# A four-layer block on one core: groups of a quantised weight loaded ahead into free rows, page copies moved into the down stage

## The reference

```python
# layer 0: gated MLP with an adapter (rank 16) per sequence, F = 1376
gate = x @ W_gate.T + 0.5 * lora(x, A_gate, B_gate)
up   = x @ W_up.T   + 0.5 * lora(x, A_up, B_up)
x = x + (silu(gate) * up) @ W_down.T + 0.5 * lora(silu(gate) * up, A_down, B_down)

# layer 1: attention, 32 query and 8 key/value heads of 128, over 512 cached keys + 128 new ones
kc = k_cache[block_table].reshape(bsz, L, HK, D)      # 16 pages of 32 keys per sequence
vc = v_cache[block_table].reshape(bsz, L, HK, D)
x = x + softmax(mask(rope(rmsnorm(q)) @ k_all.T * SCALE)) @ v_all @ Wo.T

# layer 2: weight quantised to a codebook, per group of 128 inputs
delta = lora_B @ lora_A * 0.5
normalized = (weight + delta) / exp(scale_log)        # 4 groups
quantized = cb[searchsorted(thresholds, normalized)]
x = x + x @ ((quantized - normalized + normalized) * exp(scale_log) + delta).T

# layer 3: one of eight weights per sequence
x = x + einsum('bsi,boi->bso', x, weight[adapter_ids])
```

## Time and profile before

| | us |
|---|---|
| median of 3 runs | 1441.49 |
| lowest, highest | 1437.01, 1442.73 |
| profiled execution | 1439.98 |
| its span | 1438.4 |
| PE busy in it | 1378.1 (96%) |
| DVE, ACT, POOL busy | 1021.5, 977.4, 744.6 |

### The profile page before, as it was taken

How to read it: one execution, slowest core, us unless ns; L and a number is a source line. 1 busy time by engine, 2 the same in 40 slices (tenths; PEclk the granted TensorE clock), 3 DMA queues, 4 the chain that set the end, 5 groups by cost and what they waited for, 6 DMA issues and landing times.

```text
span 1438.4 us, 26330 instructions
## 1 busy us (share of the span) xinstructions
PE 1378.1 (96%) x7812; PEld 1190.9 (83%) x7812; DVE 1021.5 (71%) x2111; ACT 977.4 (68%) x1986; POOL 744.6 (52%) x986
## 2 busy tenths in 40 slices
PE   6899898889999999999999999999999999999888
PEld 5788776678888888888888888888888888888766
DVE  3787666467777777777777777777777777777656
ACT  4667564467777677777776777777777777777643
POOL 5322222376666566656555665565566656655300
PEclk9999999999999999999999999999999999999989
DMA  8788778356332424332332324232323242422144
GB/s 193 220 268 271 238 183 268 96 141 177 88 89 59 105 58 111 67 103 68 80 104 60 90 76 113 62 89 60 103 60 89 73 114 53 100 60 59 33 180 147
DMA packets 256596, 165.80 MB, mean 115 GB/s; under 512 B 157398, under 2 KB 223575, under 8 KB 250951
## 3 DMA queue, kind: packets, MB, share of 16 engines
q1 hardware_dynamic: 250928, 144.51, 37.3%
q0 software_dynamic: 5376, 19.60, 4.8%
q10 hardware_dynamic: 150, 0.01, 0.0%
HBM read 158.66 MB, written 38.94 MB: 137 GB/s over the span
## 4 chain that ended last, share of the span: by engine, by line
PE 74%; DVE 6%; issue 5%; ACT 5%; DMA 4%; POOL 3%; SPq 2%; POOLq 0%; DVEq 0%; ACTq 0%
PE proj_ps L1361 17%; PE sc L1401 13%; PE o_ps L1439 13%; PE ring L1419 8%; PE sc L1161 5%; PE proj_ps L1455 4%; PE proj_ps L1458 3%; PE proj_ps L1466 3%; PE o_ps L1161 3%; PE proj_ps L1161 2%; DMA prep<-scale_dram 2%; PE ring L1478 1%; DMA inv_row<-inv_dram 1%; SPq L333 1%; DVE bias L1904 1%
## 5 line engine op out<-in xcount | busy, mean ns | idle before, releaser
L1921 DVE TENSOR_TENSOR pTl<-ring,pTh 128x512 fp32r<-128x512 f32 x320 | 215.3, 689 | 145.0 <-ACT pTh L969 140.8
L958 ACT ACTIVATE p_sb<-p_sb,bias,rstd 128x640 f32<-128x640 f32 x256 | 235.3, 920 | 57.6 <-DVE bias L1904 57.6
L1888 DVE CUSTOM_DVE_ANT_0 p_sb<-sc,mask 128x640 f32<-128x640 f32 x256 | 206.5, 823 | 24.4 <-PE sc L1401 18.1
L704 POOL TENSOR_TENSOR rstd<-var,half_neg 128x4 f32<-128x4 f32 x64 | 65.1, 1017 | 301.5 <-DVE var L1953 301.5
L969 ACT ACTIVATE pTh<-ring 128x512 fp32r<-128x512 f32 x320 | 184.3, 599 | 28.5 <-PE ring L1419 27.0
L1419 PE MATMUL ring<-ident,p_sb 128*128 128x128 f32 x1280 | 182.3, 273 | 4.2 <-DVE pTl L1921 2.7
L1361 PE MATMUL proj_ps<-wh,xh 128*128 128x512 f32 (+1 forms) x512 | 179.5, 351 | 0.7 <-ACT q_sb L1005 0.7
L1361 PE MATMUL proj_ps<-wl,xh 128*128 128x512 f32 (+1 forms) x512 | 173.5, 339 | 6.9 <-DVE wl L1745 6.9
L1419 PEld LDWEIGHTS ring<-ident,p_sb 128*128 128x128 f32 x1280 | 153.5, 141 | 31.1 <-DVE pTl L1921 3.2
L1361 PE MATMUL proj_ps<-wh,xl 128*128 128x512 f32 (+1 forms) x512 | 172.4, 337 | 0.0
L1401 PE MATMUL sc<-kTh,qTh 128*128 128x320 f32 x512 | 163.3, 319 | 3.0 <-DVE kTl L1995 3.0
(11 more groups left out here) (244 smaller groups left out, 3602.4 us busy)
## 6 DMA issues: line engine op xcount, KB each, us to landing
k_pages<-in_k_cache SPq DMA_DIRECT2D x128, 128.0 KB, 3.5
v_pages<-in_v_cache POOLq DMA_DIRECT2D x128, 128.0 KB, 3.7
k_raw<-k_pages SPq DMA_DIRECT2D x256, 64.0 KB, 2.5
v_raw<-v_pages SPq DMA_DIRECT2D x64, 256.0 KB, 2.9
rope<-rope_dram SPq DMA_DIRECT2D x64, 256.0 KB, 3.4
inv_row<-inv_dram SPq DMA_DIRECT2D x64, 256.0 KB, 3.7
stage<-in_Wqkv SPq DMA_DIRECT2D x32, 384.0 KB, 4.5
w_raw<-in_WguT SPq DMA_DIRECT2D x19, 512.0 KB, 5.3
```

The costliest lines, as they stand in the source:

```text
L704: pool.tensor_tensor(rstd[:, u.k % 2, 0:REP], var[:, u.k % 2, 0:REP], half_neg[:, 0:REP], ALU.pow).then_inc(S["q_pow"], 1)
L958: act_e.activation(p_sb[:, p_slot(u, h), :], p_sb[:, p_slot(u, h), :], ACT.Exp, bias=bias[:, h:h + 1], scale=rstd[:, u.k % 2, h:h + 1], ac ...
L1888: v.tensor_tensor_reduce(out=p_sb[:, p_slot(u, h), :].rearrange("p (s k) -> p s k", s=2), in0=score_ps[h % 2][:, :, 0:SPLIT], in1=mask[:, ...
L1921: v.tensor_tensor(pTl[:, c, :], ring[c % 2][:, :], pTh[:, c, :].bitcast(F32), ALU.subtract).then_inc(S["ptl"], 1)
```

## The change

**Groups in rows of their own.** Group 0 stays in `prep` 0 to 2. Groups 1 and 3 go to rows 3 to 5 of `rope_tab`, seen as `spare`, group 2 to its rows 0 to 2. Results go to `prep` rows 2, 1, 0 and 2 (`made_row`). `load_group` stands at q = 11, 13, 16 and 20 and waits for the group before to have landed; group 3 also for `leaf_step` 5, which is stage 0 of group 2. `store_group` of groups 0 and 1 moves ahead of the page copies of q = 16 and 19, group 2's behind the last copies of the loop, group 3's to n = 6 of the down loop.

**x later.** The first half of x is loaded at q = 18 instead of 13, the second at n = 3 of the down loop instead of q = 16.

**Pages.** Key pages: `KEY_COPIES` gives 2 for q 6 to 10, 3 for 11 to 15, 5 for 16 to 21, then 5, then 5 per block of the down loop instead of 2, then 5 per step of attention. Value pages: 3 instead of 5 for iterations 11 to 15, then 28 instead of 18 after gate/up.

**The down stage.** The loads of the first attention unit move two blocks (`Wqkv`, keys), or one (values, tables, `Wo`) down. On DVE stage 1 of group 3 moves from ahead of block 2's split to behind it, stage 2 from k = 3 to 4. ACT's wait for the stored results moves from k = 5 to 7.

**SBUF.** `xh`, `woh`, `wol` and `w2_h`, `w2_l` change their places in the layout.

```diff
+KEY_COPIES = [0] * 6 + [2] * 5 + [3] * 5 + [5] * 6
+        def group_row(g, n):
+            return prep[:, n, :] if g == 0 else spare[:, 3 * (g % 2) + n, :]
+        def made_row(g):
+            return prep[:, (2, 1, 0, 2)[g], :]
...
                 else:
-                    sp.wait_ge(S["w2_ready"], g)
-                load(prep[:, 0, :], ins["W2T"][:, g, :], S["w2_in"])
+                    sp.wait_ge(S["w2_in"], 48 * g)
+                    if g == 1:
+                        sp.wait_ge(S["rope_in"], 16)
+                    if g == 3:
+                        sp.wait_ge(S["leaf_step"], 5)
+                load(group_row(g, 0), ins["W2T"][:, g, :], S["w2_in"])
...
-                if q == 13:
-                    load(x_sb[:, 0:HALF, :], ins["x"][0:HALF].rearrange("b t n -> t b n"), x_in[0])
-                if q == 16:
-                    sp.wait_ge(S["xl_set"], 2 * C)
-                    load(x_sb[:, HALF:, :], ins["x"][HALF:].rearrange("b t n -> t b n"), x_in[1])
+                if q in (13, 16, 20):
+                    load_group({13: 1, 16: 2, 20: 3}[q])
                 if 19 <= q:
                     load_wd(CH + q - 19)
-                copy_keys(2 if q < FC else 5)
-                if q in (16, 19, 21):
+                if q == 18:
+                    load(x_sb[:, 0:HALF, :], ins["x"][0:HALF].rearrange("b t n -> t b n"), x_in[0])
+                if q in (16, 19):
                     store_group(q // 3 - 5)
-                    load_group(q // 3 - 4)
+                copy_keys(KEY_COPIES[q])
             copy_keys(5)
...
-            for n in range(FC):
-                if n >= 3:
-                    load_wd(CH + n)
-                    copy_keys(2)
-                if n == 5:
-                    store_group(3)
-                if n == 2:
+            store_group(2)
+            for n in range(3, FC):
+                load_wd(CH + n)
+                if n == 3:
+                    sp.wait_ge(S["xl_set"], 2 * C)
+                    load(x_sb[:, HALF:, :], ins["x"][HALF:].rearrange("b t n -> t b n"), x_in[1])
+                copy_keys(5)
+                if n == 4:
                     sp.wait_ge(S["gate_up"], 4 * FC)
...
-                copy_values(4 if n < FC else 5)
+                copy_values(4 if n < FC else 3 if n < 16 else 5)
             pool.wait_ge(S["gate_up"], 4 * FC)
-            copy_values(18)
+            copy_values(28)
...
-                    if g:
-                        dve.wait_ge(S["put"], PUT_SCALES + 16 * g)
...
-            weight2(*STAGES[2 * FC - 1])
             first = Unit(0)
             for k in range(2, CH):
                 split_wd(CH + k)
                 if k == 2:
                     mask_t(1, 2)
                     low_t(1, 2)
-                if k == 3:
+                    weight2(*STAGES[2 * FC - 1])
+                if k == 4:
                     weight2(*STAGES[2 * FC])
```

More of the change, by code:

```diff
@@ L207, in cond_resid_kernel @@
         tb_raw = prep[0:PAIR, 8, :]
+        spare = rope_tab[:, :, :, :].rearrange("p k b d -> p (k b d)").rearrange("p (r n) -> p r n", n=HID)
         wd_b = [la_h[:, :, :, :].rearrange("p k c r -> p k (c r)"), act_h[:, 0:2, :]]
@@ L222, in cond_resid_kernel @@
         wl = l1_sb("wl", [P, C, QKV], F32R)
-        woh = l1_sb("woh", [P, REP, HID], F32R)
-        wol = l1_sb("wol", [P, REP, HID], F32R)
+        xh = l1_sb("xh", [P, B, C, T], F32R)
         rope = l1_sb("rope", [P, 2, 4, D])
@@ L227, in cond_resid_kernel @@
         v_raw = l1_sb("v_raw", [P, LC, D])
-        xh = l1_sb("xh", [P, B, C, T], F32R)
+        woh = l1_sb("woh", [P, REP, HID], F32R)
+        wol = l1_sb("wol", [P, REP, HID], F32R)
         xl = l1_sb("xl", [P, B, C, T], F32R)
@@ L269, in cond_resid_kernel @@
         w3_raw = l2_sb("w3_raw", [P, 2, C, HID])
+        w2_h = l2_sb("w2_h", [P, C, HID], F32R)
+        w2_l = l2_sb("w2_l", [P, C, HID], F32R)
         x2T_h = l2_sb("x2T_h", [P, 2, C * T], F32R)
@@ L274, in cond_resid_kernel @@
         w3_h = l2_sb("w3_h", [P, 2, C, HID], F32R)
-        w2_h = l2_sb("w2_h", [P, C, HID], F32R)
-        w2_l = l2_sb("w2_l", [P, C, HID], F32R)
         w3_l = l2_sb("w3_l", [P, 2, C, HID], F32R)
@@ L388, in load_group @@
                 else:
-                    sp.wait_ge(S["w2_ready"], g)
-                load(prep[:, 0, :], ins["W2T"][:, g, :], S["w2_in"])
-                load(prep[:, 1, :], scale_dram[0, g, :].partition_broadcast(P), S["w2_in"])
-                load(prep[:, 2, :], scale_dram[1, g, :].partition_broadcast(P), S["w2_in"])
+                    sp.wait_ge(S["w2_in"], 48 * g)
[4 more added lines that the diff above has]
+                load(group_row(g, 0), ins["W2T"][:, g, :], S["w2_in"])
+                load(group_row(g, 1), scale_dram[0, g, :].partition_broadcast(P), S["w2_in"])
+                load(group_row(g, 2), scale_dram[1, g, :].partition_broadcast(P), S["w2_in"])
             def store_group(g):
                 sp.wait_ge(S["w2_ready"], g + 1)
-                sp.dma_start(w2_dram[:, g, :], prep[:, 4, :]).then_inc(S["put"], 16)
+                sp.dma_start(w2_dram[:, g, :], made_row(g)).then_inc(S["put"], 16)
             load_x_chunk(0, 0)
@@ L486, in _ @@
                     load_k(first)
-                if n == 4:
+                if n == 5:
                     load_v(first)
@@ L490, in _ @@
                     load_rope(first)
-                if n in (6, 8):
-                    for h in (n - 6, n - 5):
+                if n == 6:
+                    store_group(3)
+                if n in (7, 9):
+                    for h in (n - 7, n - 6):
                         sp.wait_ge(S["wqkv_l"], h + 1)
@@ L526, in step @@
                     load_v(u + -1)
-                if 2 <= u.k < B - 1:
+                if u.k < B - 1:
                     copy_keys(2)
                 spread_inv(u + -2)
+                if u.k < 2:
+                    copy_keys(3)
                 if (u + 1).exists():
@@ L534, in step @@
                 load_next_out(u)
-                if u.k < B - 1:
-                    copy_keys(6 if u.k < 2 else 4)
+                if 2 <= u.k < B - 1:
+                    copy_keys(3)
             run_steps(step)
@@ L930, in _ @@
                 split_wd(CH + k)
-                if k == 5:
+                if k == 7:
                     act_e.wait_ge(S["put"], PUT_SCALES + 16 * C)
@@ L1702, in weight2 @@
             def weight2(g, stage):
-                w, scale, norm, delta = (prep[:, n, :] for n in range(4))
+                w, scale, norm = (group_row(g, n) for n in range(3))
+                delta = prep[:, 3, :]
                 tmp = w
@@ L1726, in weight2 @@
                     then(v.tensor_tensor(tmp, tmp, scale, ALU.mult))
-                    v.tensor_tensor(leaf[0], tmp, delta, ALU.add).then_inc(S["w2_ready"], 1)
+                    if g == 3:
+                        dve.wait_ge(S["put"], PUT_SCALES + 16)
+                    v.tensor_tensor(made_row(g), tmp, delta, ALU.add).then_inc(S["w2_ready"], 1)
             def low_act(n):
```

## The result

| | before | changed kernel |
|---|---|---|
| median of the runs | 1440.65 us (1437.01 to 1442.73, 4 runs) | 1455.33 us (1452.7 to 1457.98, 4 runs) |
| ratio, 95% interval | | 1.0113 [1.0095, 1.0132] |
| profiled execution | 1439.98 us | 1454.83 us |
| TensorE's first product of down block 1 | 227.76 us | 216.13 us |
| down stage ended (first product of attention) | 265.10 us | 279.93 us |

The changed kernel is slower by 1.1%, 14.7 us by the medians and 14.85 us in the profiled executions. The forecast was 1453 us, in a range of 1442 to 1461. TensorE enters the down stage 11.6 us earlier, leaves it 14.8 us later, and what follows (attention and the last two layers) takes as long as before: 1173.3 us from attention's first product to the end in both.

A forecast was written before the change was run, and what follows sets the result against it. SP's page copies at 1.25 us each were taken to delay the W_down blocks: 212.3 + 51.8 issues block 10 at 264.1, the stage ends at 276.7, +11.5 us, so 1441.5 + 11.5 = 1453 us, range 1442 to 1461.

The forecast's parts named there:

- What bounds: Whole run: TensorE works in nearly all of attention, so moving the down stage's end moves the run by as much.
- Part 1, -8.9 us: Gate/up: loading groups ahead removes DVE's scale-row waits and TensorE's resulting waits, so TensorE enters the down stage 8.9 us earlier.
- Part 2, at most -5.3: Down stage: weight2 behind the W_down split removes at most TensorE's 3.6 us wait and 1.7 us of low clock.
- Part 3, 1.25 us a page: SP queue, down loop: each page costs 1.25 us, so a block comes every 6.85 us or later; TensorE uses two in 5.75.
- The start, load 4 at 212.3: Down stage: load 4 waits for DVE's split of block 1, 10.0 us earlier at 212.3; SP arrives at the same moment, 211.6.
- The sum, 51.8 us to block 10: SP queue: issues and pages from load 4 take 51.8 us, so block 10 is issued at 264.1 instead of 254.76.
- "Six or seven us from one `wd_raw` issue to the next": SP queue, down stage: sign that the forecast is right; issues closer than 6 us would show it wrong.
- The tail, 12.5 us: Down stage after block 10's issue: 10.5 us as in the trace, plus 2 us for the late Wo loads.
- The end of the stage, 276.7: Down stage ends at 276.7 instead of 265.26, +11.5 us; bounds +6.5 and +16.
- What costs nothing: GpSimd's 28 value pages after gate/up end at 246, before the stage ends; fewer attention pages gain at most 1 or 2, taken as 0.
- The rival "faster": Down stage: the queue is no bound, TensorE alone sets the stage, ending at 250.7, a run of 1427; chance 0.12.
- Hold-ups like the 3.11 us: SP queue, down stage: rival slower by more, five transfer hold-ups of 2.5 us, +12.5 more, 1465; chance 0.06.

The follow-up runs named there:

- the nine kernels: The kernel before (1440.65 us), the changed kernel (1455.33 us) and the seven experiment kernels, measured from 1426.73 to 1464.63 us.
- the one with the low stretch at 122 us: Kernel with key pages at their old places, its 16 down-loop pages moved into the first half of gate/up: 1426.73 us, ratio to before 0.9934.
- the run with the old `weight2` order: Kernel with key pages at their old places, VectorE's two late weight2 steps put back ahead of the block 2 and 3 splits: 1429.33 us, ratio to before 0.9943.
- the run with fixed numbers: Changed kernel with the down loop's 40 page copies taken from constant page numbers, none read: 1436.91 us, ratio to before 0.9993.
- the run of the pages alone: Kernel before with only the key pages moved as in the change: 1464.63 us, ratio to before 1.0188.
- the first four experiments: Changed kernel with old key-page places 1429.99 us, small copies 1451.51, fixed page numbers 1436.91; kernel before with only key pages moved 1464.63.

## Why the prediction was right, step by step

**What bounds.** Right. A change of the down stage's end went through to the run one to one: 14.8 us at the stage's end, 14.8 in the span. That rests on what follows, which took 1173.3 us in both; that it agrees so closely is in part luck, since over the nine kernels it lies between 1168.3 and 1173.3 (last section).

**Part 1, -8.9 us.** (Its own terms make 8.8.) The mechanism was right and the size near. Down block 1 began 11.6 us earlier. Of that, 2.0 us was there at 120 us already, ahead of the waits that I had counted: TensorE's product that waits for `e_sb` there starts at 121.40 us before and at 119.43 now. The low clock lies differently in the two executions: 0.79 from 40 to 48 us before, where the changed kernel has 1.00, and 0.76 from 33 to 40 us now, where the kernel before has 1.00 and TensorE more idle time. Counted from that product, block 1 begins 106.4 and 106.1 us later in the two kernels with the old groups, and 96.7 or 96.8 in six of the seven with groups ahead (98.3 in the one with the low stretch at 122 us). So the part won 9.3 to 9.7 us. VectorE's first operation on each group now comes directly behind its predecessor. SP's new waits for groups cost the weight blocks nothing, as taken.

**Part 2, at most -5.3.** I left this inside the sum, as a wait that begins earlier. It is worth nothing that can be measured even where the raw blocks are there (the run with the old `weight2` order). The 2.1 us of the earlier trace rows were VectorE's, four operations and two Wqkv parts ahead of a low half; the move takes them away and puts 2.0 before another block.

**Part 3, 1.25 us a page.** Right: from block 9's issue at 258.28 to the end of its five pages at 265.22 it is 6.94 us, for 6.85 forecast. That the number's reading is half of it was read from a gap in the trace of before, and the run with fixed numbers shows it.

**The start, load 4 at 212.3.** It left at 210.89, 1.4 us earlier, and not for the reason I gave. VectorE had split block 1 by 209.97 (209.28 + 0.69), 2.3 us before the forecast, by the extra gain of part 1. What load 4 waited for was SP itself: the five pages ahead of it ended at 210.85, for 211.6 forecast. I had SP and VectorE arrive together; here the queue is already the later of the two. With fixed numbers VectorE is the later: the split ends at 210.76 and the load leaves at 210.79.

**The sum, 51.8 us to block 10.** It was 55.5, and block 10 was issued at 266.36, not 264.1. The term that was mis-sized is the four Wqkv and four k loads: 4.2 forecast, 6.0 measured (2.28 + 3.68, with the gap between), where the kernel before had 1.77 + 2.40. Why they take longer was not tried; in the run with fixed numbers the k loads take 4.27. The long issue behind them I had: 3.11 us in the earlier trace rows, 3.23 now. The remaining 1.9 us lie in small places: `v_raw` 0.95 instead of 0.6, the gaps before the pages, five pages of 5.91 behind block 8.

"Six or seven us from one `wd_raw` issue to the next" held only for the bare pages (7.1 us behind block 8); with the other loads between it was 7.6 to 12.9.

**The tail, 12.5 us.** 13.6 us, and the two parts of it are not the ones I named. From block 10's issue to its first product it took 6.3 us (266.36 to 272.65); before, 5.6 (254.76 to 260.34). ScalarE did stand 7.2 us for the last two Wo rows, but that costs 0.7, not 2. From the first product to the end of the stage it took 7.3 us, before 4.8: the products ran at the low clock. ScalarE's timeline, and four windows behind TensorE's stops of 7.2, 3.1, 4.1 and 6.9 us before blocks 6, 7, 8 and 10 (the clock stands third from the right):

```profile
269.04 0.63 ACT L860 ACTIVATE woh<-stage 128x512 fp32r<-128x512 f32 x1 [7.17 <-DMA stage<-in_WoT]
270.00 0.63 ACT L860 ACTIVATE woh<-stage 128x512 fp32r<-128x512 f32 x1 [0.33 <-DMA stage<-in_WoT]
...
271.01 0.62 ACT L839 ACTIVATE wd_h<-wd_raw 96x512 fp32r<-96x512 f32 x1
```

```profile
241.90:244.90 3.00, 3.00 (x7) 2.42 (x8) 0.00 (x0) 0.00 (x0) 0.97 (x2) 0.50 0.92 251
249.90:252.80 2.90, 2.90 (x12) 2.11 (x12) 0.00 (x0) 0.00 (x0) 0.00 (x0) 1.00 0.64 164
257.00:262.20 5.20, 5.20 (x12) 3.96 (x13) 0.30 (x1) 0.63 (x1) 0.00 (x0) 0.50 0.45 128
272.70:277.90 5.20, 5.20 (x12) 3.94 (x13) 1.37 (x2) 2.73 (x5) 0.00 (x0) 0.50 0.37 107
```

After three of the four stops the products run at the lower level (1.2 instead of 2.4 GHz), after the 3.1 us before block 7 at the full one. As long as the next block is late anyway, the low clock is free; behind block 10 nothing is late, and its twelve products take 5.5 us where the same took 2.9 at full clock, 2.6 lost. I had this as a bound of 1.7 us and not in the sum. The landings were as sized: 2.9 to 6.4 us, median 4.6, against the earlier trace rows. The formula of the Trainium skill ("DMA: Bandwidth & Descriptors", Anatomy of one DMA), fitted for GpSimd's path, makes an estimated 2.6 us, less than the shortest of these loads from SP, so it did not hold for them.

**The end of the stage, 276.7.** 279.9, 14.8 us over before, where 11.5 was the forecast and +16 the upper bound: -1.4 from the start, +3.7 from the sum and +1.1 from the tail are the 3.3 us over the forecast, within rounding. So the total was nearer than its parts: the start was forecast 1.4 us too late, which hid part of the rest. The lower bound of +6.5 does not come out of its terms: block 10 had landed in 2.9 us in the kernel before too, so 11.5 - 2.5 - 2 = 7.0. TensorE's waits before blocks 6 to 10 were 7.2, 3.1, 4.1, 0 and 6.9, where "4 to 6" each stood: 21.3 together, in 20 to 30. Of the 15 to 25 us of waits on `wd_raw`, TensorE's were 23.5 in the whole stage and ScalarE's 25.1.

**What costs nothing.** GpSimd's last page of the 28 was issued at 244.96, for 246 forecast. With ten key pages less in attention, what follows the stage took 1173.3 us as before, and 1171.6 in the run of the pages alone: no gain beyond the spread of the last section.

**The rivals.** The queue was a bound, as the first four experiments show. The rival "faster" describes the kernel without pages in the down loop: 10.7 us under before, for 14.6. Its stage took 34.7 us where the rival had 31.8 (250.7 less 218.9); 2.0 of the difference is the wait before block 3, behind `weight2`. Hold-ups like the 3.11 us came once, not five times. The groups were ahead.

## What to carry to other kernels

A copy whose address is read from a table costs its queue the read as well as the issue, here 1.25 us for 128 KB or for 8 KB alike; count such instructions against the time in which the consumer uses up one of the blocks queued among them, here 2.9 us, before moving them. A busy queue can pay for such an instruction elsewhere too: spread the copies where the consumer has a buffer's worth of slack, and check the next stage for the 2 or 3 us that come back. And when one change holds a gain and a loss, test the four corners; here the start and the length of the stage were additive to within 1 us, and half of the change is the better kernel.

## What was not expected of the hardware

The last stage of the run has a stretch at the low clock in some kernels' profiled executions and not in others, with the same instructions. The windows (columns as in the earlier trace rows) are of the kernel before, of the changed kernel, and of the kernel with the pages at their old places; each begins 1095 to 1100 us after the first product of attention. The third lies 5 us earlier than the others by this count; in the 5 us behind it the clock is 1.00 too.

```profile
1365.00:1385.00 20.00, 14.98 (x57) 11.38 (x57) 9.94 (x10) 8.16 (x9) 0.00 (x0) 0.78 0.63 215
```

```profile
1380.00:1400.00 20.00, 13.97 (x49) 10.45 (x47) 9.18 (x10) 7.20 (x7) 0.00 (x0) 0.74 0.57 215
```

```profile
1350.00:1370.00 20.00, 11.86 (x62) 9.10 (x61) 11.28 (x13) 10.57 (x14) 0.00 (x0) 1.00 0.50 171
```

From attention's first product to the end these executions took 1173.3, 1173.3 and 1169.9 us. Of the nine kernels' executions, four have 10 us there at a mean clock of 0.66, and took 1171.6 to 1173.3; the five without took 1168.3 to 1170.7. The stretch costs some 3 us, less than 20 us at 0.74 to 0.78 would, since TensorE stood for 5 to 6 of them. With one profile per kernel it is not shown whether the kernel or the execution decides. The 17 runs of the kernel before on one chip differ too, from 1432.7 to 1443.2 us at a mean granted clock of the whole run between 0.987 and 0.994, so I take the execution as the likelier. It is why the comparisons above go by the end of the down stage, and why a span alone is no better than 5 us here.
